# Writing out the loop over the fourteen middle batches of an attention and convolution kernel

## What is computed

```
q = transpose(x) @ Wq.T                       # (16, 1024, 512), 8 heads of 64
logits = (scale * q q^T * cmask + (1 - cmask) * NEG) * rmask    # masks from cond
x = x + transpose((softmax(logits) q) @ Wo.T)
x = x + causal depthwise conv(x, w=cond, 16 taps, along the 512) + b
```

## Time and profile before

| | |
|---|---|
| three runs | 4293.75, 4297.24, 4297.84 us; median 4297.24 |
| span of the profiled execution | 4288.0 us, first to last instruction |
| PE busy | 4140.9 us, 97% of the span |
| ACT, POOL, DVE busy | 2849.5, 2602.8, 2495.8 us (66%, 61%, 58%) |
| DMA | 385.34 MB, mean 90 GB/s |
| granted TensorE clock, mean | 0.994 |

### The profile page before, as it was taken

How to read it: one execution, slowest core, us unless ns; L and a number is a source line. 1 busy time by engine, 2 the same in 40 slices (tenths; PEclk the granted TensorE clock), 3 DMA queues, 4 the chain that set the end, 5 groups by cost and what they waited for, 6 DMA issues and landing times. The chain is left out here.

```text
span 4288.0 us, 56952 instructions
## 1 busy us (share of the span) xinstructions
PE 4140.9 (97%) x18688; PEld 2978.4 (69%) x18688; DVE 2495.8 (58%) x2260; ACT 2849.5 (66%) x3905; POOL 2602.8 (61%) x1044
## 2 busy tenths in 40 slices
PE   7999999999999999999999999999999999999799
PEld 4776767677676767767676776767677676767598
DVE  4664555556455655645565565556556565655676
ACT  4775767667576766757676675767667576766465
POOL 4775757667576766757676675757667575766300
PEclk8999999999999999999999999999999999999999
DMA  3323333232333323233333323333332333332488
GB/s 103 82 67 71 80 83 94 69 89 65 72 80 81 94 71 87 65 74 80 79 94 73 85 65 76 79 77 94 75 84 67 77 79 75 94 74 60 128 283 269
DMA packets 286191, 385.34 MB, mean 90 GB/s; under 512 B 148947, under 2 KB 217171, under 8 KB 285782
## 3 DMA queue, kind: packets, MB, share of 16 engines
q1 hardware_dynamic: 285910, 381.57, 34.9%
HBM read 112.28 MB, written 67.11 MB: 42 GB/s over the span
## 5 line engine op out<-in xcount | busy, mean ns | idle before, releaser
L698 POOL TENSOR_TENSOR plo<-p,phi 128x1024 fp32r<-128x1024 f32 x1024 | 2597.5, 2548 | 1405.1 <-ACT phi L628 1390.2
L742 DVE TENSOR_REDUCE mrow<-misc 128x1 f32<-128x1024 f32 x1024 | 1215.0, 1218 | 1076.9 <-PE misc L470 1073.2
L626 ACT ACTIVATE p<-sc 128x512 f32<-128x512 f32 x2048 | 1109.9, 594 | 848.7 <-PE sc L509 622.6
L522 PE MATMUL pv<-phi,val 128*128 128x512 f32 x4096 | 1136.1, 399 | 42.2 <-issue 42.2
L628 ACT ACTIVATE phi<-p 128x1024 fp32r<-128x1024 f32 x1024 | 1086.6, 1061 | 32.5
L522 PEld LDWEIGHTS pv<-phi,val 128*128 128x128 f32 x4096 | 766.5, 188 | 252.1 <-issue 76.6
L508 PE MATMUL sc<-quer,keys 128*128 128x512 f32 x2048 | 916.8, 448 | 22.9 <-issue 17.5
L509 PE MATMUL sc<-quer,keys 96*128 96x512 f32 x2048 | 810.1, 396 | 0.0
L526 PE MATMUL pv<-plo,val 128*128 128x512 f32 x2048 | 648.3, 397 | 0.7 <-POOL plo L698 0.7
L470 PE MATMUL misc<-quer,keys 128*128 128x512 f32 x2048 | 599.9, 401 | 23.4 <-DMA keys<-lo 11.7
L508 PEld LDWEIGHTS sc<-quer,keys 128*128 128x128 f32 x2048 | 386.3, 189 | 199.9 <-issue 75.0
(11 more groups left out here) (67 smaller groups left out, 2646.8 us busy)
## 6 DMA issues: line engine op xcount, KB each, us to landing
keys<-hi SPq DMA_DIRECT2D x256, 256.0 KB, 3.1
quer<-mhi SPq DMA_DIRECT2D x256, 256.0 KB, 4.4
keys<-lo SPq DMA_DIRECT2D x128, 256.0 KB, 4.9
quer<-mlo SPq DMA_DIRECT2D x128, 256.0 KB, 3.8
xo<-x SPq DMA_DIRECT2D x64, 512.0 KB, 3.9
x<-xo SPq DMA_DIRECT2D x64, 512.0 KB, 5.0
xin<-x SPq DMA_DIRECT2D x16, 2048.0 KB, 13.4
out<-stage SPq DMA_DIRECT2D x64, 512.0 KB, 6.4
```

Of the source, the lines that this page charges most:

```text
L522: pe.matmul(pv[:, half(h)], val[:, i, t, part, :], phi[:, t % NPHI, half(h)], start=(t == 0 and part == 0), stop=False)
L626: act.activation(p32[:, t % NP32, half(h)], sc[:, h, :], ACT.Exp, scale=SCALE).then_inc(s_p32, 1)
L698: pool.tensor_tensor(plo[:, t % NPLO, :], p32[:, t % NP32, :], phi[:, t % NPHI, :].bitcast(F32), ALU.subtract).then_inc(s_plo, 1)
L742: reduced = dve.tensor_reduce(mrow[:, q:q + 1], misc[:, k, :], AX.X, ALU.max)
```

## The change

```
@@ -299,7 +299,7 @@
             start()
             batch("first", 0)
-            with eng.Fori(1, B - 1) as b:
+            for b in range(1, B - 1):
                 batch("mid", b)
             batch("last", B - 1)
             end()
```

## The result

The changed kernel takes 4312.22 us (median of 5 runs, 4311.86 to 4315.03), the kernel before 4296.99 (5 runs). The ratio is 1.004 with a 95% interval of [1.0028, 1.0051]: 0.4% slower, where 0.49% had been forecast. The profiled execution has a span of 4310.2 us and took 4311.89, so 1.7 us lie around its span.

What follows compares the result with a forecast made beforehand. PE, 97% busy, was taken as the bound. Fourteen written-out batches of 251.2 us (3516.8 against 3495.8) add 21.0 to the span of 4288.0; 9.2 more gives 4318.2 us, 0.49% slower, range 4311 to 4324.

Steps and rivals of the forecast that it cites:

- What bounds the kernel, and the stretches as a ruler: PE, 97% busy, bounds; lengths between score matmuls in already written-out batches price a middle batch at 251.2 us, before 249.7.
- The port: POOL's subtraction starts before DVE's `lo` in pairs 0, 2 and 3, i = 0; PE loses 1.61 us or a little more.
- The branch: At the loop's end on PE: removing the taken branch gains 1.5 us, thirteen times, 19.5 us.
- The register instructions on PE: PE's four matmuls for maxima at t = 1 take 1.19 us without them, 1.43 in the loop: 0.24 us.
- The rival with DVE first: DVE's `lo` stays ahead of POOL, branch and register delays gone: 4244.7 us, between 4250 and 4226; chance 0.04.
- The runs' median stands 9.2 us above the span: Around the whole execution: 9.2 us added to the predicted span of 4309.0 us, giving 4318.2.
- The counts: `lo` 3.4 us long in 48 of 64 executions, 1.2 in the rest; DVE's busy time up by 92 us.

Runs made afterwards that it cites:

- pe_only: Kernel before with only PE's loop written out, the other four engines keeping theirs; 4275.49 us, ratio 0.9949.
- dve_first: Changed kernel plus one POOL wait, so DVE's `lo` starts first in stretches with i = 0 of pairs 0, 2 and 3; 4251.32 us.
- df_loop_act: dve_first with the loop put back on ACT; 4268.39 us, ratio 0.9935 to the kernel before.
- df_loop_pool: dve_first with the loop put back on POOL; 4252.29 us, ratio 0.9896 to the kernel before.
- the second profile: The kernel before, unchanged, run and profiled once more; one run of 4297.64 us, span 4295.9, middle batches 3501.0.
- loop_pool_act: Changed kernel with the loop put back on POOL and ACT; 4275.33 us, ratio 0.9953 to the kernel before.
- pool_only: Kernel before with only POOL's loop written out, the other four engines keeping theirs; 4344.4 us, ratio 1.0111.
- act_only: Kernel before with only ACT's loop written out, the other four engines keeping theirs; 4342.47 us, ratio 1.0112.
- not_pe: Kernel before with ACT, POOL, DVE and SP written out and PE keeping its loop; 4340.28 us, ratio 1.0101.

## Why the prediction was right, and where it wasn't

- **What bounds the kernel, and the stretches as a ruler.** Right. The written-out stretches of the kernel before gave 251.2 us a batch; measured 251.15 (3516.1 / 14), or 251.25 without the one stretch of batch 14 that went the other way.
- **The port.** Right, and shown by both directions: forced to DVE's good it gives 60.9 us back, and taken from DVE by POOL's or by ACT's written-out program alone it costs 47 to 48 us. The Trainium skill (SBUF — State Buffer, section Who interferes with whom) says that a VectorE instruction with two SBUF inputs contends with a GpSimd instruction that reads SBUF, at a shared read interface, and that the engine that issues first has the shared ports for its whole instruction. The traces agree: `lo` takes 3.4 or 1.22 us and nothing between, in every kernel, and a start ahead by 0.02 to 0.05 us decides it. They show the exclusion; that it is this port rather than some other resource only the Trainium skill says.
- **The branch.** Right in place and size: 1.5 us a batch. Written out on PE alone the kernel gains 21 us, 18 in the middle against the first profile, 23 against the second. The Trainium skill (Runtime: NRT & Kernel Launch, section Instruction fetch mechanics) says that a taken branch can stall the fetch of instructions, and that this is one reason to prefer full unrolling. The trace agrees on the stall (3334 ns taken, 83 not; that it is the fetch, no run shows); unrolling pays in pe_only (4275.49 us) and dve_first (4251.32), where DVE stays first, and not in the changed kernel, where it doesn't.
- **"The register instructions on PE".** The size was right, the owner wrong. The 0.24 us at t = 1 are ACT's, which frees the bank late (df_loop_act, df_loop_pool). It made no difference to the sum, since that was taken from whole stretches.
- **The rival with DVE first.** 4244.7 was worked out with 1.75 us a stretch; the price is 1.42 (31.99 against 30.57), and dve_first takes 4251.3. The prediction had put the price at 1.61 at least, what PE lost between two of its operations; the whole stretch lost less than that, so dve_first lies above the 4226 to 4250 given for this case. Its 1.61 "or a little more" was wrong for the forecast too, but the sum there was taken from whole stretches.
- **The step that failed in size** is "The runs' median stands 9.2 us above the span". What lies around a span is 1.7 us, in every run. The profiled execution of before had been a short one: 4288.0 us, where 4291.4 to 4296.9 were the spans of the same kernel's runs beside the experiments. So the 21.0 us were reckoned against an execution that wasn't an ordinary one, and the forecast of 4318.2 came out 6 us too high; the measured 4312.2 lies just inside the range, 1.2 us above its lower end. Against the second profile the middle batches differ by 3516.1 - 3501.0 = 15.1 us, and the medians by 15.2. The branch stalls and the clock's falls behind them vary from run to run, and with PE written out both are gone from the middle batches.
- **The counts.** 47 long `lo` instead of 48 (batch 14). DVE's busy time rose by 99.5 us, where 92 had been forecast; 41 x 2.217 = 90.9 of it are `lo`, and 4.6 are the normalisation (L778), 210.3 us instead of 205.7.

## What to carry to other kernels

When two engines share a resource that one operation holds to its end, look at who starts first and by how much: here 0.08 us of register instructions a tile, on an engine that is nowhere near the bound, were worth 1.1%. If the order matters, write it down with a semaphore instead of leaving it to the instructions around it; with that one wait, writing out the loop went from 0.4% slower to 1.0% faster. And if a kernel holds both forms of a code already, the stretches of its own trace price a change better than a sum of instructions does; but check that the profiled execution is one of the ordinary ones before adding a difference to it.

## What the runs showed of the hardware that was not expected

- The order at the port is decided on the scale of 0.02 us, and repeats: 42 of 42 stretches in loop_pool_act with DVE ahead by 0.02 us, 42 of 42 in pool_only with POOL ahead by 0.05.
- With PE looped the granted TensorE clock fell to 0.5 (the level of 1.2 GHz) for 3.4 us behind some of the branches: twice in the second profile of the kernel before (at 1521 and 2023 us), three times each in act_only (522, 1536, 2550) and not_pe (1537, 2045, 3059), never in the first profile and in pool_only. PE had stood idle for 1.6 to 2.9 us just before each fall, and the stretch was 1.5 us longer. But the idle time alone doesn't tell: behind 1.68 us in the first profile, 1.71 in act_only and 1.89 in not_pe the clock stayed up. With PE written out it never fell in the middle batches.
- In all six kernels with ACT written out, ACT's exponential in stretch (0, 0) of batch 14 came 0.28 us late, as shown above for one; in the four of them without the forced order DVE won this one stretch by it. It was late in none of those with ACT looped. That it goes with a place in ACT's written-out program is shown by this; what makes it late there was not tried.
